# Layer 3's expert weights fetched per block by SyncE instead of held in SBUF, and batch 0's tokens ranked and scattered between the two layer 2 parts

## What is computed

```
q, k, v = split(x @ w_qkv.T)                  # 64 wide, causal softmax attention
s = softmax(q k^T / 8, causal) v @ w_out.T + b_out
logits = x @ router_w.T                       # 16 experts, top 2, softmax of the two
out_e = (silu(x @ gate_e) * (x @ up_e)) @ down_e      # inner width 64
ffn = sum of the two chosen experts, weighted, + a shared expert
x = x + s * silu(ffn)
```

## Time and profile before

| | |
|---|---|
| median of 3 runs | 818.15 us (818.07 to 821.54) |
| profiled execution, device time | 818.05 us |
| its span, first to last instruction | 816.0 us |
| mean granted TensorE clock | 0.84 of 2.4 GHz |
| PE busy (matmul) | 708.3 us, 87% |
| DVE, ACT, POOL busy | 413.3, 380.6, 266.4 us |
| layer 2 of batch 0; BETWEEN; layer 2 of batch 1; FINAL | 295 to 431; to 502; to about 632; to 816 |

### The profile page before, as it was taken

How to read it: one execution, slowest core, us unless ns; L and a number is a source line. 1 busy time by engine, 2 the same in 40 slices (tenths; PEclk the granted TensorE clock), 3 DMA queues, 4 the chain that set the end, 5 groups by cost and what they waited for, 6 DMA issues and landing times. The chain is left out here.

```text
span 816.0 us, 13289 instructions
## 1 busy us (share of the span) xinstructions
PE 708.3 (87%) x4280; PEld 478.7 (59%) x4280; DVE 413.3 (51%) x918; ACT 380.6 (47%) x907; POOL 266.4 (33%) x255
## 2 busy tenths in 40 slices
PE   5999978999989994899987999779897889799982
PEld 2775523898666662666654655456675666466660
DVE  1737633564345375588635365557874333221245
ACT  5404567345774433475745524347575533142231
POOL 2000181072730037665510000856642070160042
PEclk9958989899999997999977769789999977755565
DMA  8900020276442122000000001110020131332122
GB/s 320 281 1 0 7 97 27 79 238 198 128 127 77 52 78 59 35 14 2 1 1 0 1 2 54 57 37 14 2 53 1 39 110 33 94 87 64 39 58 72
DMA packets 53025, 53.90 MB, mean 66 GB/s; under 512 B 8792, under 2 KB 40960, under 8 KB 52576
## 3 DMA queue, kind: packets, MB, share of 16 engines
q1 hardware_dynamic: 47936, 41.64, 16.7%
q0 software_dynamic: 5024, 11.41, 4.6%
HBM read 36.36 MB, written 16.68 MB: 65 GB/s over the span
## 5 line engine op out<-in xcount | busy, mean ns | idle before, releaser
L1283 ACT ACTIVATE arena<-bank 128x512 f32<-128x512 f32 (+7 forms) x224 | 119.4, 538 | 179.2 <-PE bank L681 93.0
L1283 ACT ACTIVATE arena<-bank,arena 128x128 f32<-128x128 f32 (+1 forms) x244 | 87.9, 386 | 102.3 <-PE bank L681 36.3
L681 PE MATMUL bank<-arena 128*64 128x128 f32 (+7 forms) x944 | 129.2, 357 | 3.2 <-ACT arena L1283 2.2
L681 PEld LDWEIGHTS bank<-arena 128*64 128x64 f32 (+4 forms) x944 | 84.3, 175 | 41.4 <-issue 17.1
L681 PE MATMUL bank<-arena,w 128*128 128x512 f32 (+2 forms) x208 | 91.2, 571 | 4.6 <-ACT arena L1283 4.6
L681 PE MATMUL bank<-w_ew,arena 128*128 (+1 forms) x512 | 72.2, 288 | 0.6 <-ACT arena L1283 0.3
L681 PEld LDWEIGHTS bank<-w_ew,arena 128*128 128x128 f32 x512 | 67.8, 206 | 2.1 <-issue 1.3
L2576 POOL DMA_INDIRECT slots_in<-arena x32 | 33.3, 1039 | 101.7 <-ACT arena L1283 92.2
L681 PEld LDWEIGHTS bank<-arena,w 128*128 128x128 f32 (+1 forms) x208 | 37.5, 198 | 36.0 <-issue 24.8
L2668 POOL TENSOR_TENSOR arena<-arena 128x512 f32<-128x512 f32 x32 | 33.3, 1041 | 72.3 <-DVE arena L2293 72.3
L2676 POOL TENSOR_TENSOR arena<-arena,const 128x512 f32<-128x512 f32 x32 | 51.1, 1598 | 10.1 <-ACT arena L1283 10.1
(11 more groups left out here) (252 smaller groups left out, 1182.9 us busy)
## 6 DMA issues: line engine op xcount, KB each, us to landing
work<-in_ew SPq DMA_DIRECT2D x46, 256.0 KB, 3.0
work<-decays SPq DMA_DIRECT2D x16, 264.0 KB, 3.5
slots_in<-work SPq DMA_DIRECT2D x2, 2048.0 KB, 20.2
work<-slots_in SPq DMA_DIRECT2D x16, 256.0 KB, 2.8
slots_out<-arena SPq DMA_DIRECT2D x16, 256.0 KB, 2.3
arena<-slots_in SPq DMA_DIRECT2D x10, 256.0 KB, 3.6
slots_out<-arena POOLq DMA_DIRECT2D x10, 256.0 KB, 3.3
w_ew<-in_ew SPq DMA_DIRECT2D x1, 2048.0 KB, 11.6
```

What stands on the lines that cost most here:

```text
L681: return nc.tensor.matmul(o, lhsT, rhs, start=start, stop=stop, skip_group_check=True)
L1283: return nc.scalar.activation(o, i, f, bias=bias, scale=scale, **kw)
```

## The change

The expert weights of layer 3 are no longer held in SBUF. `order_weights3` copies them from DRAM to DRAM in the order wanted (gate and up in 256 byte pieces, down in 512 byte pieces; four DMAs on SP's queue between layer 1's blocks and batch 0's decays). `load_weights3` on SP loads a block's expert to a register and fetches its 64 KB of gate and up and its 32 KB of down weights into a ring three groups deep; a group is 4 register loads and 8 DMAs, and waits until the group three back has been used (`eo3`). It stands ahead of `load_rows3` in SP's loop. In `first` the weights become the stationary operand and the rows the moving one, so the hidden layer comes out transposed: `inner`, its ACT copy and PE's register loads go. Two blocks share a bank on partition halves: even blocks 0 to 63, odd ones 64 to 127, in `first` as output columns of the array, in `second` as its input rows. An advance of the PE stream now does turned(i), first(i-1), second(i-2): 10 advances a batch. Batch 0's R0 comes earlier in `BETWEEN`, and POOL issues its 16 scatters there, ahead of batch 1's layer 2. The lists lose empty advances.

```diff
-    "scatter": [0, 2, 3, 4],
...
-BETWEEN = ("T1", "E0", "T1", "A0.0", "E0", "T1", "A0.0", "T1", "E0", "A0.0", "T1", "E0", "A0.0", "N1", "A0.0", "N1", "R0",
-           "A0.0", "N1", "A0.0", "A0.1", "N1", "A0.0", "R0", "A0.1", "A0.0", "N1", "R0", "A0.1", "U0.0", "N1", "A0.1", "U0.0",
-           "A0.1", "U0.1", "A0.1", "U0.1", "A0.1", "A0.1", "A0.1")
+BETWEEN = ("T1", "E0", "T1", "E0", "A0.0", "T1", "E0", "A0.0", "R0", "T1", "E0", "A0.0", "R0", "T1", "A0.0", "R0", "A0.0", "N1",
+           "A0.0", "N1", "A0.1", "A0.0", "N1", "A0.1", "A0.0", "N1", "A0.1", "U0.0", "N1", "A0.1", "U0.0", "N1",
+           "A0.1", "U0.1", "A0.1", "U0.1", "A0.1", "A0.1")
...
+                def load_weights3(n, q):
+                    j = n * NQ3 + q
+                    if j >= RING3:
+                        sp.wait_ge(*at_of((j - RING3) // NQ3, "eo3", (j - RING3) % NQ3))
+                    for i in range(SB):
+                        e = nc.values_load(block_e3[0:1, n, q * SB + i:q * SB + i + 1], engines=[mybir.EngineType.SP],
+                                           min_val=0, max_val=(E3 - 1) * P)
+                        half = slice(i % 2 * H3, (i % 2 + 1) * H3)
+                        sp.dma_start(ring_pair[:, j % RING3, i].rearrange("p a h -> p (a h)"),
+                                     pairs3[:, bass.ds(e, P)]).then_inc(ring3_sem[j % RING3], 16)
+                        sp.dma_start(ring_down[half, j % RING3, i // 2], downs3[:, bass.ds(e, P)]).then_inc(
+                            ring3_sem[j % RING3], 16)
...
+                order_weights3()
                 for n in range(B):
                     put_decays(n)
...
-                    for q in range(NQ3 + 5):
+                    for q in range(NQ3 + 4):
+                        if q == 0:
+                            sp.wait_ge(*at_of(n, "block_e3"))
                         if q < NQ3:
+                            load_weights3(n, q)
                             load_rows3(n, q)
-                        if q >= 5:
-                            store_rows3(n, q - 5)
+                        if q >= 4:
+                            store_rows3(n, q - 4)
...
                     def first(q):
-                        o = fresh("quick", "pair3", q)
-                        pe.wait_ge(*at("cols3", q))
-                        for i in range(SB):
-                            e = expert(q, i)
-                            j = mm(o[:, cs(i)], cols3[:, q % 2, cs(i)], W3["pair"][:, bass.ds(e, 2 * H3)])
-                        j.then_inc(*step("pair3", q))
+                        og, ou = fresh("quick", "gate3b", q), fresh("quick", "up3b", q)
+                        j = n * NQ3 + q
+                        pe.wait_ge(ring3_sem[j % RING3], 16 * 2 * SB * (j // RING3 + 1))
+                        pe.wait_ge(*at("cols3", q))
+                        for p in range(SB // 2):
+                            for a, o in enumerate((og, ou)):
+                                for i in (2 * p, 2 * p + 1):
+                                    last = mm(o[i % 2 * H3:(i % 2 + 1) * H3, cs(p)], ring_pair[:, j % RING3, i, a],
+                                              cols3[:, q % 2, cs(i)])
+                        last.then_inc(*step("up3b", q))
...
                     def second(q):
-                        o = fresh("slow", "eo3", q)
+                        outs = [fresh("slow", "eo3_" + side, q) for side in ("even", "odd")]
                         pe.wait_ge(*at("hhb3", q))
                         for i in range(SB):
-                            e = expert(q, i)
-                            j = mm(o[:, cs(i)], hhb3[:, q % 2, cs(i)], w_down3[:, bass.ds(e, P)])
-                        j.then_inc(*step("eo3", q))
+                            half = slice(i % 2 * H3, (i % 2 + 1) * H3)
+                            last = mm(outs[i % 2][:, cs(i // 2)], hhb3[half, q % 2, cs(i // 2)],
+                                      ring_down[half, (n * NQ3 + q) % RING3, i // 2])
+                        last.then_inc(*step("eo3", q))
...
+                for _ in range(C):
+                    advance("R0")
                 now[:] = [2, 1]
                 layer2()
```

More of the change, by code:

```diff
@@ L454, in four_layers @@
         rows_out3 = take([2, SB, P])
-        tgb3 = take([2, SB, H3])
-        hb3 = take([2, SB, H3])
-        hhb3 = take([2, SB * P], H3)
+        tgb3 = take([2, SB * H3])
+        hb3 = take([2, SB * H3])
+        hhb3 = take([2, SB * H3])
         fetched3 = [w_ew2[:, 2 * T:].rearrange("p (c k d) -> p c k d", k=2, d=P), take([2 * C, 2, P])]
@@ L475, in four_layers @@
         scattered3 = [sem(f"scattered3_{n}") for n in range(B)]
+        ring3_sem = [sem(f"ring3_{i}") for i in range(RING3)]
         rows_in3_sem = [sem(f"rows_in3_{i}") for i in range(2)]
@@ L545, in _, with order_weights3 @@
                 head, shared = columns(PACK3[0:5])[1], columns(PACK3[8:])[1]
-                pair = W3["pair"].rearrange("p (e a h) -> p e a h", a=2, h=H3)
                 sp.dma_start(w3t[:, 0:head], p3[:, 0:head]).then_inc(ready["three"], 16)
-                for i, name in enumerate(("gate", "up")):
-                    sp.dma_start(pair[:, :, i], given3[name].rearrange("p (e h) -> p e h", h=H3)).then_inc(ready["three"], 16)
                 sp.dma_start(w3t[:, -shared:], p3[:, -shared:]).then_inc(ready["three"], 16)
                 sp.dma_start(w_out3[:], wout3).then_inc(ready["three"], 16)
+                def order_weights3():
+                    for i, name in enumerate(("gate", "up")):
+                        sp.dma_start(pairs3.rearrange("p (e a h) -> p e a h", a=2, h=H3)[:, :, i],
+                                     given3[name].rearrange("p (e h) -> p e h", h=H3)).then_inc(ready["down"], 16)
+                    for i in range(2):
+                        sp.dma_start(downs3.rearrange("h (e a d) -> h e a d", a=2, d=P)[:, :, i], given3["down"][
+                            i * H3:(i + 1) * H3].rearrange("h (e d) -> h e d", d=P)).then_inc(ready["down"], 16)
+                def load_weights3(n, q):
[10 more added lines that the diff above has]
+                            ring3_sem[j % RING3], 16)
                 def load_rows(q):
@@ L1720, in blocks3 @@
                     act.wait_ge(*at_of(1, "x", 3, 1))
-                    for i in range(NQ3 + 2):
+                    for i in range(NQ3 + 1):
                         if i < NQ3:
@@ L2479, in blocks3 @@
                     yield
-                    for i in range(1, NQ3 + 3):
+                    for i in range(1, NQ3 + 2):
                         if i <= NQ3:
                             q = i - 1
-                            pair = psum("pair3", q)[:].rearrange("p (b a k) -> p b a k", b=SB, a=2)
-                            h = hb3[:, q % 2]
                             after(("tgb3", q))
+                            v.scalar_tensor_tensor(hb3[:, q % 2], tgb3[:, q % 2], 1.0, psum("gate3b", q)[:, 0:SB * H3], ALU.add,
+                                                   ALU.mult).then_inc(*step("gate3b", q, "read"))
+                            after()
                             if n or q >= 2:
                                 b, before = before3(n, q)
-                                dve.wait_ge(*at_of(b, "ht3", before))
-                            v.scalar_tensor_tensor(h, tgb3[:, q % 2], 1.0, pair[:, :, 0], ALU.add, ALU.mult).then_inc(*step())
-                            after()
-                            v.scalar_tensor_tensor(h, h, 0.5, pair[:, :, 1], ALU.mult, ALU.mult).then_inc(*step("hb3", q))
-                            reached[("pair3", q, "read")] = reached[("hb3", q)]
-                        if i >= 3:
-                            q = i - 3
+                                dve.wait_ge(*at_of(b, "eo3", before))
+                            v.scalar_tensor_tensor(hhb3[:, q % 2], hb3[:, q % 2], 0.5, psum("up3b", q)[:, 0:SB * H3], ALU.mult,
+                                                   ALU.mult).then_inc(*step("hhb3", q))
+                            reached[("up3b", q, "read")] = reached[("hhb3", q)]
+                        if i >= 2:
+                            q = i - 2
                             after(("eo3", q))
@@ L2497, in blocks3 @@
                                 dve.wait_ge(rows_out3_sem[q % 2], 16 * ((n * NQ3 + q) // 2))
-                            v.tensor_copy(rows_out3[:, q % 2], psum("eo3", q)[:].rearrange(
-                                "p (b d) -> p b d", d=P)).then_inc(*step("rows_out3", q))
-                            reached[("eo3", q, "read")] = reached[("rows_out3", q)]
+                            for a, side in enumerate(("even", "odd")):
+                                v.tensor_copy(rows_out3[:, q % 2, a::2], psum("eo3_" + side, q)[:, 0:SB // 2 * P].rearrange(
+                                    "p (b d) -> p b d", d=P)).then_inc(*step("rows_out3", q))
+                                reached[("eo3_" + side, q, "read")] = reached[("rows_out3", q)]
                         yield
```

(3 more changed lines are left out.)

61 lines of the change are left out of this document (20 added, 41 removed).

## The result

The changed kernel takes **867.66 us** (median of 4 runs, 860.69 to 874.09) against 818.41 (818.07 to 821.54, 4 runs): ratio 1.0564, 95% interval 1.0483 to 1.0646. Runs over 1.5% above the fastest of their kernel, which show a lower granted clock, are left out of every ratio, so it can differ a little from that of the medians. Forecast: 849, range 822 to 874, and in its sum a narrower own range of 835 to 862, which the result misses by 6 us.

A forecast was written before the change was run, and what follows sets the result against it. PE bounds the kernel, with waits in layer 3's expert blocks and at batch 1's layer 2. 818.05 - 10 (scatter) + 1 (copies) + 10.9 (B0) + 29.5 (B1) = 849 us, range 822 to 874.

The forecast's parts named there:

- The closed loop: Layer 3: PE's advance, SP's 6.0 us of weights and 3.1 for the rows follow one another, without overlap, from q = 3.
- SP's pass, 6.0 us: Layer 3: SP issues a group's weights in four blocks of 1.50 us, of which 0.40 is the second DMA.
- rival 4: Layer 3: rows land late behind the eight weight DMAs, at 5.1 us, 2.1 more a loop: 873 us; chance 0.07.
- The advance, 4.2 us at half clock: Layer 3: PE's transposes 0.9, column halves 2.2 and row halves 1.1 us a group, against 7.0 in all before.
- Rival 3: Layer 3: products on the two halves do not overlap, 1.9 us more a loop: 874 us; chance 0.12.
- Rival 2: Layer 3: SP takes 6.0 us but PE runs at the full clock, period 11.2: 820 us; chance 0.06.
- rival 1: Layer 3: SP's pass is quick, 3.7 us, and the clock stays up, loop 8.9: 792 us; chance 0.08.
- rival 5: Layer 2 gives nothing back, DVE and ACT taking over PE's waits: 859 us; counted with the forecast, no separate chance.
- The period of B1, 13.3: Layer 3, batch 1: five loops of 9.1 + 4.2 us each; B1 itself brings +29.5 us.
- B0, +10.9: Layer 3, batch 0: five advances of 9.1 + 3.6 us, clock between two levels, end it at 718.0 against 707.1.
- The scatter, -10: Batch 1's layer 2: moving 16 scatters out removes both PE waits, 8.8 us; 10 us gained, bounds 5 and 15.
- The DRAM copies, +1: SP's queue ahead of batch 0's decays: copying expert weights loses 1 us, bounds 0 and 6.

The follow-up runs named there:

- two one-line edits: Changed kernel with SP loading a group's rows ahead of its weights: ratio 0.9881; or, separately, with the ring four groups deep: ratio 0.9806, both to the kernel before.
- experiment 3: Kernel before, layer 3 untouched, 16 scatters ahead of batch 1's layer 2: ratio 1.0007; with the change's BETWEEN order too: 0.9903, repeated at the 820 level 0.9864.
- experiments 7: Changed kernel with one weight DMA a block in place of two, weights still ahead of rows: 831.13 us, ratio 1.0104 to the kernel before.
- 8: Changed kernel, one weight DMA a block, rows first: 773.17 us, ratio 0.9447; also two DMAs, rows first, four ring places: 783.22 to 800.11 us.
- the later run in 3: Kernel before with the scatters ahead of batch 1's layer 2 and the change's BETWEEN order, at the 820 level: 809.47 us, ratio 0.9864.
- Experiment 5: Changed kernel with a group's products reordered, all of one partition half and then all of the other: 916.61 us, ratio 1.0676 to the kernel before.

## Why the prediction was right, and by how much it was off

The direction and the mechanism were right, the measured time is inside the range, and the point was 18.7 us low (15.8 against the profiled execution). In the trace, 15.4 us more were lost than the sum has: 4.9 ahead of B0's third advance, 7.3 in B0, 2.4 in B1, 0.8 behind it. None of the four cancels another, so the range held by its width; the own range of 835 to 862 did not hold.

- **The closed loop** (rows q not issued before SP's pass, SP's pass not before `eo3` of q-3): right. It is seen in the timelines, and either of two one-line edits opens it.
- **SP's pass, 6.0 us: too small.** Measured 6.7. I priced the second DMA of a block by the first's 0.33; it costs 0.485, with its register work 0.56 and not 0.40, and a block 1.66 and not 1.50. This is the mis-sized term. Rows 3.1 us after issue: right at the median, with 3.5 at most; rival 4 (5.1) is out.
- **The advance, 4.2 us at half clock: right** at 3.9 to 4.1, and so is the half clock (0.50 to 0.62 in the windows). Rival 3 is out, and its price was twice too high: without neighbours on different halves the advance is 0.9 longer. Rival 2 is out by the windows, rival 1 by the pass of 6.7 us and the period, rival 5 by the 8.2 us that layer 2 gave back. Rival 4's price does not follow from its own numbers: 5.1 - 3.1 = 2.0 us of loop, at 13.4 us of time for each, are 27 and not 24, and give 876, above the range.
- **The period of B1, 13.3: measured 14.2.** The difference is SP's 0.7 and some 0.2 of semaphores between the engines, which I had at nothing. B1 came to +31.9 against +29.5: the five periods sum to 69.0 and not 66.5, the first of them being only 12.1. That B1 came out within 2.4 us is in part luck: its first rows came 1.9 late, and the pieces around the five periods took 1.9 less than I gave them.
- **B0, +10.9: measured +18.2.** The largest error. I took periods of 12.7, with attention pieces keeping the clock between its levels. They came every 13.1 to 14.4 us, like those of B1, with the transposes at half clock in all five; the five sum to 69.8 and not 63.5, which is 6.3 of the 7.3 us.
- **The scatter, -10: right as a net in the part measured alone** (11 us, experiment 3), but in the changed kernel's trace it is -8.2 in layer 2 and +5.9 ahead of it, which I had at 0 with 3 either way. Ahead of layer 2 PE waits 3.25 and 4.29 us for ACT, which now does R0's pieces in between:

```profile
455.84 1.08 PE L1148 MATMUL bank<-const,arena 128*128 128x128 f32 x4 [3.25 <-ACT arena L1295]
...
474.46 3.59 PE L703 MATMUL bank<-w,xn_a 128*128 128x32 f32 x16 [4.29 <-ACT arena L1295]
```

  These waits are not the whole cause: the traces of experiments 7, 8 and of the later run in 3 have them too (4.93 and 4.29), and there the stretch is only 1.9 to 2.7 us longer than before. What sets the changed kernel's trace apart is PE's busy time in it, 64.0 against 58.7 to 59.0 us, at a granted clock of 0.75 against 0.80 to 0.82. Why the clock was lower there stays open. In layer 2 the wait of 4.38 is 2.08 now, that for POOL of 4.46 is gone, and the scatters lie from 452.5 to 473, as said.
- **The DRAM copies, +1: 0.** They landed within 6.3 us, SP was free at 279.9, and DVE's first scan of batch 0 started at 297.56 after 0.20 us for POOL, as in the earlier trace rows. The Trainium skill (DMA: Bandwidth & Descriptors, Specifications) asks for 512 bytes at least; the copies in 256 byte pieces cost the kernel nothing, since nobody waits for them. Their price by themselves was not measured.
- **A microsecond of period for 13.4 us of time: right.** Experiment 5 adds 0.9 and costs 11 us, experiment 7 takes 2.6 and gains 33 to 38 (its ratio against the two of the changed kernel, which are of other rounds).

## What to carry to other kernels

When a load moves onto a queue, look at what stands behind it there and at what frees its buffer: if the next input of the consumer is issued after loads that wait for that consumer, the times add up instead of overlapping, and neither the queue's share nor the bytes show it. Issue the input that the consumer needs first ahead of the prefetch, or give the ring one more place, then count what the queue spends on each DMA and lay data out so that one does. A wait removed from a stretch is worth more than its length where the clock then stays up, so time it over the whole stretch.

## What the runs showed of the chip

- The kernel before took 818 to 820 us in three rounds of measurement and 860 in two. In the trace of the kernel before in a slower round ACT stands still 44.3 us in all, ended by what the profile calls remote, up to 13.3 us at a time. Every trace of the slower rounds has such waits on ACT (28.5 to 50.4 us), none of the others has one.
- A dynamic DMA into 64 partitions (32 KB) held SP longer (0.485 us) than one into 128 partitions of 64 KB or 128 KB (0.337, 0.338).
- The 16 scatters of a batch, issued with nothing between them, took POOL 20.5 us (452.5 to 473.0), 1.27 us from one to the next.
- Products on alternating column halves ran 1.45 times as fast as one half after the other (1.98 against 2.88 us for eight); for row halves the order made no difference (1.23 both).
- With eight constant products in each gap the clock was granted at 0.87 to 1.00 in B1, where it had been 0.50 to 0.62.
